# Third link of the block inverse in 64x64 products with a block diagonal operand, odd heads back from the exchanged halves one link sooner

## The chip, the cores and the metric

The kernel runs on one core of one Trainium2 chip. The metric is the device time of one execution in microseconds; lower is better. TensorE is written PE below, VectorE DVE, ScalarE ACT, GpSimd POOL, and the queue that issues most transfers SP.

## The reference, cut to what matters

A block of attention with a linear memory, followed by a gated MLP, for 4 sequences of 2048 tokens of width 256. The part that the change touches is the memory's delta rule: for each chunk of 64 tokens and each head, a strictly lower triangular 64x64 matrix is inverted, and the inverse corrects the values.

```
A0 = -jnp.where(strict, jnp.einsum('bnid,bnjd->bnij', wk, wk) * L[:, None], 0.0)
A = jnp.linalg.inv(eye - A0)
...
def step(S, inp):
    A_i, v_i, wk_i, rkg_i, wkg_i, intra_i = inp
    v_corr = A_i @ v_i
    wk_corr = A_i @ wk_i
    v_new = v_corr - wk_corr @ S
    o_i = rkg_i @ S + intra_i @ v_new
    S = gamma_C * S + wkg_i @ v_new
    return (S, o_i)
...
h = jax.nn.silu(_tlin(x, w1_w, w1_s)) * _tlin(x, w2_w, w2_s)
h = jax.nn.gelu(_tlin(h, h1_w, h1_s), approximate=False)
h = jax.nn.gelu(_tlin(h, h2_w, h2_s), approximate=False)
return _tlin(h, w3_w, w3_s)
```

## The kernel before, in words

The 32 chunks are 32 steps of a pipeline. In one step four sequences and four heads are worked on together: two sequences lie in partitions 0 to 63 and 64 to 127 (the chain `c`), and the 8 pairs of the other sequence bit and head are the index `m`, where `m` below `NP` = 4 are even heads (`e` = 0) and the rest odd heads (`e` = 1). So there are 16 matrices of 64x64 in a step, and each diagonal half of one is a 32x32 block; a 32 partition quarter is `quarter(c, i)`.

The order of the work is written out by hand in lists. `mixed` is the list of steps 3 to 33: the MLP of one chunk (`l1`, `l2` of this step, `l3` and `y` of the step before) is interleaved on PE with the small products of the memory for the next chunks. Each engine walks the same list and takes its own part of each item. A column of `l2` is 16 matmuls of 128x256. The items around the change come in this order in `mixed`: after column 7 of `l1` comes `lead`, after `l2` column 2 `join`, after `l2` column 4 `n` 3 and then `state`, after `l2` column 6 `attn_out`. `lead` and `join` serve two chunks: they finish one and start the inverse of the next.

The inverse of a 32x32 block is a product of three links. `lead` makes the first term (`first_term`, line 1120), DVE's `step_part` copies and transposes it. `join` makes square and term (`square_and_term`, line 1124) in quarters of 32x32, between the corner products (line 1146). DVE's `first_part` (lines 881, 882, 885) turns the square, subtracts the term, and adds the unit matrix. `n` 3 (line 1352) is the third link: 32 products of 32x32, one for each quarter of each matrix. ACT's `block_diagonal` (line 720) copies the result out of PSUM into `diag`, which holds the two 32x32 blocks of a matrix on a 64x64 diagonal. `state` follows at once on PE (lines 1420 and 1422), 32 products of 64x64.

A product whose operands lie in partition half `c` can write its result into the other half. In `mixed`, `first_term` does so for all heads, so that links one and two work in exchanged halves, and `move_inverse` has SP bring the block inverses into the exchanged halves too. The third link brings the result back.

PSUM tiles: `duo0` and `duo1` have two banks each, `solo0`, `solo1`, `mlp0`, `mlp1` one each. A product in fp32 is two LDWEIGHTS and two MATMUL in the trace; so 32 products of line 1352 are 64 rows there.

Of the kernel before, what the change touches and what calls it, by code (L numbers as in the profile page):

```python
# [22 lines left out]
F32 = mybir.dt.float32  # L23
# [3 lines left out]
ACT = mybir.ActivationFunctionType  # L27
# [3 lines left out]
P = 128  # L31
# [9 lines left out]
HB = C // 2  # L41
# [24 lines left out]
CO_TURN = CO_UP + C  # L66
CO_ROW = CO_TURN + P
CO_UNIT = CO_ROW + P
CO_N = CO_UNIT + HB


CHECKS = {0: (0,), 1: (1,), 2: (2, 3, 4), 3: (5,), 4: (6,), 5: (7, 8, 9, 10)}
# [5 lines left out]
def constants():  # L78

    c = np.zeros((P, CO_N), np.float32)  # L80
    p = np.arange(P)[:, None]
    j, i = p % C, np.arange(C)[None, :]
    c[:, CO_ID:CO_ID + P] = np.eye(P)
    c[:, CO_EYE:CO_EYE + SB] = j % SB == np.arange(SB)[None, :]
    c[:, CO_SUB:CO_SUB + HB // SB] = j % HB // SB == np.arange(HB // SB)[None, :]

    c[:, CO_MASK:CO_MASK + C] = (j // SB == i // SB) & (j > i)

    c[:, CO_MASK + C:CO_MASK + 2 * C] = (j // HB == i // HB) & (j // SB < i // SB)

    c[:, CO_MASK + 2 * C:CO_MASK + 3 * C] = (j >= HB) & (i < HB)
    c[:, CO_BLK:CO_BLK + 2] = j // HB == np.arange(2)[None, :]
    c[:, CO_UP:CO_UP + C] = i > j
    c[:, CO_DIST] = np.abs(p[:, 0] - (C - 1))

    c[:, CO_TURN:CO_TURN + P] = (p // C == p.T // C) & (j + j.T == C - 1)
    c[C - 1, CO_ROW:CO_ROW + P] = 1.0
    c[:, CO_UNIT:CO_UNIT + HB] = j % HB == np.arange(HB)[None, :]
    c[:, CO_E] = np.e
    return c  # L100


def half(k):
    return slice(C * k, C * k + C)
# [16 lines left out]
def main(nc, ctx, sb, sem, sems, x, wts, wv, wr, wmod, cT, scales, s3, decay, const, out):  # L121
# [30 lines left out]
    xin = sb("xin", [NB, D])  # L152
    last = sb("last", [NB, D])
    slot_low = sb("slot_low", [SLOTS // UNIT_SLOTS])
    any_low = sb("any_low", [1])
    row_low = sb("row_low", [1])


    NPAIR = H // 2
# [1 line left out]
    with ExitStack() as early:  # L161
        wmod_sb = sb("wmod_sb", [KT, 6 * D], F32, early)
        cT_sb = sb("cT_sb", [KT, B], F32, early)
        scT = sb("scT", [KT, B], F32, early)
        scB = sb("scB", [KT, B, C], F32, early)
        s3_sb = sb("s3_sb", [KT], F32, early)
        gate_col = sb("gate_col", [2, KT, B], F32, early)
        sgn = sb("sgn", [2, KT, B], F32, early)
        mag = sb("mag", [2, KT, B], F32, early)
        gate_cols = sb("gate_cols", [2, KT, B, C], F32, early)  # L170
        dec = sb("dec", [NPAIR + H + NPAIR], F32, early)
        gam = sb("gam", [NPAIR + H + NPAIR], F32, early)
        edec = sb("edec", [NPAIR + H + NPAIR], F32, early)
        powers = sb("powers", [H], F32, early)
        pow_row_sb = sb("pow_row_sb", [P], F32, early)
        hank = sb("hank", [H, C], F32, early)
        low_bits = sb("low_bits", [UNIT_SLOTS * SLOT * P], F32, early)
    act_hi = [sb(f"act_hi{i}", [HK, TOK], F32R) for i in range(2)]
    act_lo = [sb(f"act_lo{i}", [HK, TOK], F32R) for i in range(2)]
# [42 lines left out]
    mi = sb("mi", [2 * NP, HB])  # L222
    step_nt = sb("step_nt", [2 * NP, HB])
    square_t = sb("square_t", [2 * NP, HB])
    first_two = sb("first_two", [2 * NP, HB])
    vn = sb("vn", [NP, 2, DH])
    o_state = sb("o_state", [NP, P])
# [244 lines left out]
    with nc.Block() as block:  # L472
# [238 lines left out]

        @block.scalar
        def _(act):
            def block_diagonal(a):

                act.wait_ge(rest_full, a + 1)
                after(act, own_full, a)
                after(act, mi_full, a)
                for i in range(2):
                    ins = act.activation(diag[:, :, HB * i:HB * (i + 1)], of_head(duo[1][:, 1, 0:2 * NP * HB]), ACT.Copy, scale=con[:, CO_BLK + i:CO_BLK + i + 1])  # L720
                ins.then_inc(diag_ready, 1)

            def new_values(a):
# [3 lines left out]
            def step(n, g, items):  # L727
                def part(name, k, a, p):
# [31 lines left out]
                        for e in range(2):  # L760
                            act.copy(gram[:, e], grams(a, e)[:, :, 0:C]).then_inc(gram_ready[e], 1)
                    if name == "n" and k == 3:
                        block_diagonal(a)
                    if name == "lead" or name == "solve" and k == 0:
                        act.wait_ge(own_full, now)
                        act.copy(vn[:].rearrange("p q e n -> p (q e n)"), solo[1][:]).then_inc(own_ready, 1)
# [66 lines left out]
        def _(dve):  # L833
# [45 lines left out]
            def first_part(a):  # L879
                dve.wait_ge(first_full, a + 1)  # L880
                dve.transpose(square_t[:].rearrange("p k n -> p (k n)"), duo[1][:, 0, 0:2 * NP * HB]).then_inc(square_turned, 1)
                dve.tensor_tensor(first_two[:], first_inv_t, of_head(duo[1][:, 0, 2 * NP * HB:4 * NP * HB]), ALU.subtract).then_inc(first_ready, 1)
                dve.wait_ge(const_in, 16)
                dve.wait_ge(square_turned, a + 1)
                dve.tensor_tensor(square_t[:], square_t[:], con[:, CO_UNIT:CO_UNIT + HB].unsqueeze(1).to_broadcast([P, 2 * NP, HB]),
                                  ALU.add).then_inc(square_ready, 1)

            def step_part(a):
                dve.wait_ge(step_full, a + 1)
# [3 lines left out]
            def step(n, g, items):  # L893
# [4 lines left out]
                def part(name, k, a, p):  # L898
# [68 lines left out]
                    if name == "lead" and (not isinstance(n, int) or n + 1 < STEPS):  # L967
                        step_part(n + 1)
                    if name == "n" and k == 2:
                        first_part(a)  # L970
                    if name == "join" and (not isinstance(n, int) or n + 1 < STEPS):
                        first_part(n + 1)
# [141 lines left out]
        def _(pe):  # L1114
# [7 lines left out]
            def square_and_term(m, rows):  # L1122

                return pe.matmul(duo[1][rows, 0, :].rearrange("p (t k n) -> p t k n", t=2, n=HB)[:, :, m, :], step_nt[rows, m, :],  # L1124
                                 step_and_inv[rows, :, m, :], start=True, stop=True)

            def inner(m, c):

# [25 lines left out]
            def step(general, n, g, items):  # L1154
# [86 lines left out]
                def part(name, k, a, p):  # L1241
# [86 lines left out]
                    if name == "n":  # L1328
                        pe.wait_ge(const_in, 16)
                        if k == 1:  # L1330
                            pe.wait_ge(cross_ready, now)
                            pe.wait_ge(inv_ready, now)
                            if items is third:
                                pe.wait_ge(state_ready, a)
                        if k == 2:
                            pe.wait_ge(step_ready, now)
                            pe.wait_ge(inv_t_ready, now)
                            if items is third:
                                pe.wait_ge(ao_scaled, a)
# [6 lines left out]
                        for e, q, c, i in quarters if k > 1 else ():  # L1346
                            rows, m = quarter(c, i), e * NP + q
                            if k == 2:
                                mm = square_and_term(m, rows)
                            if k == 3:  # L1350
                                back = quarter(1 - c if items is mixed else c, i)
                                mm = pe.matmul(of_head(duo[1][back, 1, 0:2 * NP * HB])[:, m, :], square_t[rows, m, :], first_two[rows, m, :], start=True, stop=True)  # L1352
                        mm.then_inc({1: step_full, 2: first_full, 3: rest_full}[k], 1)
                    if name == "join":
                        has_next = not isinstance(n, int) or n + 1 < STEPS
                        pe.wait_ge(const_in, 16)
                        if has_next:
                            pe.wait_ge(step_ready, n + 2)
                        pe.wait_ge(mi_ready, now)
                        pe.wait_ge(own_ready, now)  # L1360
                        pe.wait_ge(o_state_ready, a)

                        for e in range(2):
                            for q in range(NP):
                                m = e * NP + q
                                for c in range(2):
                                    last_corner = corner(m, e, q, c)
                                if has_next:
                                    for i in range(2):
                                        for c in range(2):  # L1370
                                            last_terms = square_and_term(m, quarter(c, i))
                        last_corner.then_inc(vn_full, 1)
                        if has_next:
                            last_terms.then_inc(first_full, 1)
# [50 lines left out]
                    if name == "attn_out":  # L1425
                        if items is alone:
                            pe.wait_ge(wr_ready, 1)
                        pe.wait_ge(oT_ready, now)
                        for b in range(NB):
                            for hp in range(H // 2):  # L1430
# [84 lines left out]
```

## Time and profile before

| | before |
|---|---|
| median of 3 runs | 1748.63 us |
| lowest and highest | 1748.12 and 1750.38 us |
| the profiled execution's own time | 1744.08 us |
| its span, first to last instruction | 1742.3 us |
| granted PE clock over the span | 0.991 |
| PE busy | 1716.0 us, 98% |
| DVE, ACT, POOL busy | 64%, 55%, 34% |

A step in the middle is 52.0 us long. Start times in a timeline are from the span's start; "x64" is the number of instructions that the row merges. A matmul's own duration includes the way through the array, and matmuls overlap, so what a group costs is the time from its first start to the first start of the next group.

### The profile page before, as it was taken

What the parts mean: (1) busy time and instruction counts of PE and PEld (TensorE: products, weight loads), DVE (VectorE), ACT (ScalarE), POOL (GpSimd) and SP (SyncE); (2) the same over time, 40 slices, a digit from 0 to 9 for tenths busy, and PEclk for the clock granted to TensorE, in tenths of its full rate; (3) what the DMA queues carried; (4) which work ended last, traced back from release to release, by engine and by line L of the source; (5) the groups of instructions that cost most, each with busy time, mean ns of one, the idle gap of its engine ahead of it and who ended that gap; (6) DMA issues with size and microseconds to landing.
All of it is one profiled execution on the core that took longest, in us unless ns stands there. A gap on an engine that the chain in (4) does not pass through costs nothing.

```text
span 1742.3 us, 60528 instructions
## 1 busy us (share of the span) xinstructions
PE 1716.0 (98%) x25488; PEld 1651.6 (95%) x25488; DVE 1115.4 (64%) x3041; ACT 963.3 (55%) x2249; POOL 593.5 (34%) x694
## 2 busy tenths in 40 slices
PE   8799999999999999999999999999999999999999
PEld 5698999999999999999999999999999999999998
DVE  5677666666666666676666676666666666666432
ACT  4664555555555555555555555555555555565554
POOL 3544333343333343333243333243233243243101
PEclk8899999999999999999999999999999999999999
DMA  8101000000000000000000000000000000000000
GB/s 291 68 14 33 12 23 23 18 20 11 24 23 23 18 20 11 24 23 24 17 21 15 20 23 23 20 17 19 16 23 23 21 17 21 14 23 17 8 3 12
DMA packets 37356, 47.08 MB, mean 27 GB/s; under 512 B 9236, under 2 KB 29336, under 8 KB 37080
## 3 DMA queue, kind: packets, MB, share of 16 engines
q1 hardware_dynamic: 35088, 40.75, 8.4%
q8 instruction: 206, 3.38, 0.8%
q10 hardware_dynamic: 1992, 2.38, 0.5%
q14 instruction: 70, 0.57, 0.1%
HBM read 22.53 MB, written 8.39 MB: 18 GB/s over the span
## 4 chain that ended last, share of the span: by engine, by line
PE 93%; DVE 1%; issue 1%; POOL 1%; ACT 1%; DVEq 0%; POOLq 0%
PE mlp L1163 64%; PE mlp L1235 6%; PE solo L1163 3%; PE duo L1431 3%; PE solo L1304 3%; PE solo L1136 2%; PE duo L1352 1%; PE duo L1129 1%; PE duo L1420 1%; PE solo L1440 1%; PE duo L1124 1%; PE duo L1325 1%; PE solo L1146 1%; PE duo L1422 1%; PE duo L1316 1%
## 5 line engine op out<-in xcount | busy, mean ns | idle before, releaser
L1163 PE MATMUL mlp<-act_hi,w_hi 128*128 128x256 f32 x4096 | 968.0, 283 | 1.1 <-POOL act_lo L668 0.6
L1163 PE MATMUL mlp<-act_lo,w_hi 128*128 128x256 f32 x4096 | 945.2, 277 | 0.0
L1163 PEld LDWEIGHTS mlp<-act_hi,w_hi 128*128 128x128 f32 x4096 | 770.1, 188 | 9.8 <-POOL act_lo L668 1.3
L1163 PEld LDWEIGHTS mlp<-act_lo,w_hi 128*128 128x128 f32 x4096 | 770.4, 188 | 0.8
L805 ACT ACTIVATE full<-mlp,scale_sb 128x256 f32<-128x256 f32 x512 | 246.4, 481 | 553.7 <-PE mlp L1163 553.5
L895 DVE TENSOR_TENSOR act_lo<-full,act_hi 128x256 fp32r<-128x256 f32 x512 | 240.2, 469 | 321.7 <-ACT act_hi L806 319.1
L668 POOL TENSOR_TENSOR act_lo<-full,act_hi 128x256 fp32r<-128x256 f32 x256 | 186.6, 735 | 501.9 <-ACT act_hi L795 501.9
L806 ACT ACTIVATE act_hi<-mlp,scale_sb 128x256 fp32r<-128x256 f32 x512 | 242.6, 474 | 0.0
L1163 PE MATMUL mlp<-xh,w_hi 128*128 128x256 f32 x768 | 190.8, 286 | 3.5 <-issue 3.0
L1163 PE MATMUL mlp<-xl,w_hi 128*128 128x256 f32 x768 | 189.8, 282 | 0.0
L607 POOL TENSOR_TENSOR rstd<-ve,minus_half 128x2 f32<-128x2 f32 x64 | 49.1, 768 | 331.7 <-DVE ve L844 331.3
L1014 DVE SCALAR_TENSOR_TENSOR full<-mlp,scale_sb,gate 128x256 f32<-128x256 f32 x192 | 92.8, 484 | 99.2 <-ACT gate L790 96.8
L1163 PEld LDWEIGHTS mlp<-xh,w_hi 128*128 128x128 f32 x768 | 145.9, 190 | 5.1 <-issue 4.2
L790 ACT ACTIVATE gate<-mlp,scale_sb 128x256 f32<-128x256 f32 x192 | 91.0, 474 | 107.7 <-PE mlp L1163 107.7
L1163 PEld LDWEIGHTS mlp<-xl,w_hi 128*128 128x128 f32 x768 | 146.2, 190 | 0.0
L1235 PE MATMUL mlp<-w_hi,act_hi 128*128 128x256 f32 x512 | 118.2, 277 | 0.0
L1235 PE MATMUL mlp<-w_hi,act_lo 128*128 128x256 f32 x512 | 118.1, 276 | 0.0
L607 POOL TENSOR_TENSOR rinv<-ssm,minus_half 128x8 f32<-128x8 f32 x32 | 52.8, 1650 | 182.2 <-DVE ssm L873 182.2
L795 ACT CAST act_hi<-full 128x256 fp32r<-128x256 f32 x256 | 101.7, 397 | 10.6 <-DVE full L1014 10.6
L1235 PEld LDWEIGHTS mlp<-w_hi,act_hi 128*128 128x128 f32 x512 | 96.1, 188 | 0.1
L1235 PEld LDWEIGHTS mlp<-w_hi,act_lo 128*128 128x128 f32 x512 | 96.1, 188 | 0.0
L779 ACT ACTIVATE h<-solo,sbm,cb 128x64 f32<-128x64 f32 x256 | 84.0, 438 | 0.3 <-PE solo L1440 0.3
(179 smaller groups left out, 2679.9 us busy)
## 6 DMA issues: line engine op xcount, KB each, us to landing
w_raw<-in_wts SPq DMA_DIRECT2D x22, 512.0 KB, 5.0
kg<-r SPq DMA_DIRECT2D x64, 126.0 KB
xin<-in_x SPq DMA_DIRECT2D x62, 128.0 KB
out_y<-y SPq DMA_DIRECT2D x62, 128.0 KB, 2.5
step_and_inv<-square_t SPq DMA_DIRECT2D x56, 64.0 KB, 2.0
wmod_sb<-in_wmod ACTq DMA_DIRECT2D x1, 1024.0 KB, 9.1
kg<-last SPq DMA_DIRECT2D x64, 2.0 KB
last<-r SPq DMA_DIRECT2D x64, 2.0 KB, 1.7
```

The source lines that it names most:

```text
L607: pool.tensor_tensor(dst[:], src[:], minus_half[:, 0:src.shape[1]], ALU.pow).then_inc(done, 1)
L668: pool.tensor_tensor(act_lo[0][:, k, :], full[k % 3][:], act_hi[0][:, k, :].bitcast(F32), ALU.subtract).then_inc(l_ready[0], 1)
L779: ins = act.activation(h2[:].rearrange("p k b n -> p (k b n)")[:, cols], solo[1][:, cols], ACT.Identity, bias=sbm[:, k, b:b + 1], scale=cb ...
L790: act.activation(gate[k % 2][:], gated[k % 3][:, 0:TOK], ACT.Silu, scale=scale_sb[:, 0, k:k + 1]).then_inc(l_act[0], 1)
L795: act.copy(act_hi[0][:, j, :], full[j % 3][:]).then_inc(l1_hi, 1)
L805: act.activation(full[k % 2][:], mlp[k % 2][:, 0:TOK], ACT.Gelu, scale=s)
L806: act.activation(act_hi[layer % 2][:, k, :], mlp[k % 2][:, 0:TOK], ACT.Gelu, scale=s).then_inc(l_act[layer], 1)
L895: dve.tensor_tensor(act_lo[layer % 2][:, k, :], full[k % 2][:], act_hi[layer % 2][:, k, :].bitcast(F32), ALU.subtract).then_inc(l_ready[la ...
L1014: dve.scalar_tensor_tensor(full[k % 3][:], up, s, gate[k % 2][:], ALU.mult, ALU.mult).then_inc(prod_ready, 1)
L1163: mm = pe.matmul(dst, *general_ops, start=is_first and i == 0, stop=is_last and i == 1)
L1235: mm = pe.matmul(mlp[k][:, 0:D], *ops, start=j == 0 and i == 0, stop=j == HK - 1 and i == 1)
L1304: mm = pe.matmul(solo[0][:, b * D:(b + 1) * D], hT[:, kt, b, :], wv_sb[:, kt, :], start=kt == 0, stop=kt == KT - 1)
```

## The change

Only steps whose list is `mixed` change in their work, in four ways.

- In `join`, the square and the term go to `duo0` instead of `duo1`: even heads to its first bank, odd heads to its second. The odd heads' products write into the other partition half, so that they are back where they belong one link sooner.
- DVE's `first_part` subtracts the terms of even and odd heads apart (each from the inverse that lies in its half), turns the two squares apart into `inv`, and writes `square_d`, a block diagonal 64x64 operand, in two instructions that multiply by a mask and add a masked unit matrix.
- The third link is 16 products with a 64x64 stationary operand and 32 moving columns, in place of 32 products of 32x32. Even heads go from exchanged halves to their own, odd heads stay; even heads write the first bank of `duo1`, odd heads the second.
- ACT's `block_diagonal` reads the two banks, and `attn_out`, whose result goes into the first bank of `duo1`, waits for it (`diag_ready`).

The constants get 64 more columns; `any_low` and `row_low` move into the memory that is given back after the start, and `square_d` takes new memory.

```
-                dve.transpose(square_t[:].rearrange("p k n -> p (k n)"), duo[1][:, 0, 0:2 * NP * HB]).then_inc(square_turned, 1)
-                dve.tensor_tensor(first_two[:], first_inv_t, of_head(duo[1][:, 0, 2 * NP * HB:4 * NP * HB]), ALU.subtract).then_inc(first_ready, 1)
+                if turned:
+                    for e, own_inv in ((0, first_inv_t), (1, square_t)):
+                        ms = slice(NP * e, NP * e + NP)
+                        term = duo[0][:, e, NP * HB:2 * NP * HB].rearrange("p (k n) -> p k n", n=HB)
+                        ins = dve.tensor_tensor(first_two[:, ms], own_inv[:, ms], term, ALU.subtract)
+                    ins.then_inc(first_ready, 1)
+                    for e in range(2):
+                        ins = dve.transpose(inv[:, NP * e:NP * e + NP].rearrange("p k n -> p (k n)"), duo[0][:, e, 0:NP * HB])
+                    ins.then_inc(square_turned, 1)
...
                 dve.wait_ge(square_turned, a + 1)
-                dve.tensor_tensor(square_t[:], square_t[:], con[:, CO_UNIT:CO_UNIT + HB].unsqueeze(1).to_broadcast([P, 2 * NP, HB]),
-                                  ALU.add).then_inc(square_ready, 1)
+                if turned:
+                    for i in range(2):
+                        unit_i = con[:, CO_UNIT + HB * (i + 1):CO_UNIT + HB * (i + 2)].unsqueeze(1).to_broadcast([P, 2 * NP, HB])
+                        ins = dve.scalar_tensor_tensor(square_d[:, :, HB * i:HB * (i + 1)], inv[:], con[:, CO_BLK + i:CO_BLK + i + 1], unit_i, ALU.mult, ALU.add)
+                    ins.then_inc(square_ready, 1)
...
+            def square_and_term_back(m, c, i):
+
+                to = quarter(c if m < NP else 1 - c, i)
+                return pe.matmul(duo[0][to, m // NP, 0:2 * NP * HB].rearrange("p (t k n) -> p t k n", t=2, n=HB)[:, :, m % NP, :], step_nt[quarter(c, i), m, :],
+                                 step_and_inv[quarter(c, i), :, m, :], start=True, stop=True)
...
+                        for q in range(NP) if k == 3 and items is mixed else ():
+                            for c in range(2):
+                                for m in (q, NP + q):
+                                    back = 1 - c if m < NP else c
+                                    mm = pe.matmul(duo[1][half(back), m // NP, m % NP * HB:(m % NP + 1) * HB], square_d[half(c), m, :], first_two[half(c), m, :],
+                                                   start=True, stop=True)
...
-                                            last_terms = square_and_term(m, quarter(c, i))
+                                            last_terms = square_and_term_back(m, c, i)
...
+                        if items is mixed and (not isinstance(n, int) or n + 1 < STEPS):
+                            pe.wait_ge(diag_ready, n + 2)
```

PE's program around the third link in a mixed step, before; the rows of column 4 of `l2` stand above it, `state` below. A row is one instruction, or as many as its "x" says, and counts products, not their two passes.

```order
1109 L1163 MATMUL mlp0<-act_lo0,w_full 128x256
1110 L1352 MATMUL duo1<-first_two,square_t 32x32 [waits first_ready,square_ready,const_in]
1111 L1352 MATMUL duo1<-first_two,square_t 32x32 x31
1112 L1420 MATMUL duo0<-intra1,vn 64x64 [waits vn_ready,kg_ready,const_in]
1113 L1420 MATMUL duo0<-intra1,vn 64x64 x15
1114 L1422 MATMUL duo0<-vn,kg1 64x64 x16
...
1149 L1431 MATMUL duo1<-wr_turned,o_state 128x256 [waits oT_ready]
```

And the same place after the change:

```order
1109 L1191 MATMUL mlp0<-act_lo0,w_full 128x256
1110 L1378 MATMUL duo1<-first_two,square_d 64x32 [waits first_ready,square_ready,const_in]
1111 L1378 MATMUL duo1<-first_two,square_d 64x32 x15
1112 L1453 MATMUL duo0<-intra1,vn 64x64 [waits vn_ready,kg_ready,const_in]
1113 L1453 MATMUL duo0<-intra1,vn 64x64 x15
1114 L1455 MATMUL duo0<-vn,kg1 64x64 x16
...
1149 L1466 MATMUL duo1<-wr_turned,o_state 128x256 [waits oT_ready,diag_ready]
```

The 32 products have become 16 and nothing else moved; `attn_out` has one wait more.

DVE's program from the `l2` column before `first_part` on, in the same step, before:

```order
397 L895 TENSOR_TENSOR act_lo1<-full0,act_hi1 128x256 [waits l_act1]
398 L881 STREAM_TRANSPOSE square_t<-duo1 128x256 [waits first_full]
399 L882 TENSOR_TENSOR first_two<-step_and_inv,duo1 128x256
400 L885 TENSOR_TENSOR square_t<-square_t,con 128x256 [waits square_turned,const_in]
401 L410 REGISTER_ALU [waits h_ready]
402 L869 TENSOR_TENSOR r<-h 128x512 [waits last_in]
```

And after the change:

```order
397 L917 TENSOR_TENSOR act_lo1<-full0,act_hi1 128x256 [waits l_act1]
398 L891 TENSOR_TENSOR first_two<-step_and_inv,duo0 128x128 [waits first_full]
399 L891 TENSOR_TENSOR first_two<-square_t,duo0 128x128
400 L894 STREAM_TRANSPOSE inv<-duo0 128x128 x2
401 L904 SCALAR_TENSOR_TENSOR square_d<-inv,con 128x8x32 [waits square_turned,const_in]
402 L904 SCALAR_TENSOR_TENSOR square_d<-inv,con 128x8x32
403 L414 REGISTER_ALU [waits h_ready]
404 L875 TENSOR_TENSOR r<-h 128x512 [waits last_in]
```

Three instructions have become six, and what follows them is the same.

## Rows read from the trace of the kernel before

**Rows 1.** The page: busy time by engine, PE's clock and DMA rate in 40 slices, one costly group.

```profile
PE 1716.0 (98%) x25488; PEld 1651.6 (95%) x25488; DVE 1115.4 (64%) x3041; ACT 963.3 (55%) x2249; POOL 593.5 (34%) x694
...
PEclk8899999999999999999999999999999999999999
...
GB/s 291 68 14 33 12 23 23 18 20 11 24 23 23 18 20 11 24 23 24 17 21 15 20 23 23 20 17 19 16 23 23 21 17 21 14 23 17 8 3 12
...
L1014 DVE SCALAR_TENSOR_TENSOR full<-mlp,scale_sb,gate 128x256 f32<-128x256 f32 x192 | 92.8, 484 | 99.2 <-ACT gate L790 96.8
```

**Rows 2.** Busy time of each engine in one mixed step, from link to link.

```profile
1045.55:1097.55 52.00, 52.00 (x797) 50.60 (x796) 34.43 (x94) 28.95 (x69) 18.08 (x22) 1.00 0.08 20
```

**Rows 3.** All that PE waited for between 210 and 1620 us, longest first.

```profile
PE duo L1120 <- issue: 0.7, 2, 0.4
PE mlp L1163 <- issue: 0.3, 1, 0.3
```

**Rows 4.** Timeline of PE around one third link: start, length, group.

```profile
1045.55 0.75 PE L1352 MATMUL duo<-first_two,square_t 32*32 32x32 f32 x64
1046.24 0.69 PE L1420 MATMUL duo<-intra,vn 64*64 64x64 f32 x32
1046.75 0.65 PE L1422 MATMUL duo<-vn,kg 64*64 64x64 f32 x32
1047.33 0.38 PE L1163 MATMUL mlp<-act_hi,w_hi 128*128 128x256 f32 x1
```

**Rows 5.** The link's group over the whole span, and the first and last mixed link.

```profile
L1352 PE MATMUL duo<-first_two,square_t x2048: 183/191/213, 38.6 to 1619.3; 32*32 32x32 f32 x187
...
213.03 0.75 PE L1352 MATMUL duo<-first_two,square_t 32*32 32x32 f32 x64
...
214.23 0.65 PE L1422 MATMUL duo<-vn,kg 64*64 64x64 f32 x32
...
1618.78 0.75 PE L1352 MATMUL duo<-first_two,square_t 32*32 32x32 f32 x64
...
1619.98 0.65 PE L1422 MATMUL duo<-vn,kg 64*64 64x64 f32 x32
```

**Rows 6.** Timeline of PE in the second half of one lead.

```profile
1033.95 0.23 PE L1129 MATMUL duo<-diag,far 64*64 64x32 f32 x2
1033.96 0.23 PE L1120 MATMUL duo<-inv,cross 64*64 64x32 f32 x2
1034.01 0.23 PE L1129 MATMUL duo<-diag,far 64*64 64x32 f32 x2
...
1034.77 0.23 PE L1129 MATMUL duo<-diag,far 64*64 64x32 f32 x2
```

**Rows 7.** Timeline of PE: first group of one join, and the matmul after it.

```profile
1040.59 0.24 PE L1146 MATMUL solo<-vn,mi 32*32 32x64 f32 x2
...
1041.71 0.39 PE L1163 MATMUL mlp<-act_hi,w_hi 128*128 128x256 f32 x1
```

**Rows 8.** Timeline of DVE from the first part on; in brackets idle before, and releaser.

```profile
1041.91 0.44 DVE L881 STREAM_TRANSPOSE square_t<-duo 128x256 f32<-128x256 f32 x1
1042.28 0.38 DVE L882 TENSOR_TENSOR first_two<-step_and_inv,duo 128x256 f32<-128x256 f32 x1
1042.59 0.41 DVE L885 TENSOR_TENSOR square_t<-square_t,con 128x256 f32<-128x256 f32 x1
1042.91 0.68 DVE L869 TENSOR_TENSOR r<-h 128x512 f32<-128x512 f32 x1
...
1044.72 0.43 DVE L895 TENSOR_TENSOR act_lo<-full,act_hi 128x256 fp32r<-128x256 f32 x1 [0.20 <-ACT act_hi L806]
1046.53 0.42 DVE L895 TENSOR_TENSOR act_lo<-full,act_hi 128x256 fp32r<-128x256 f32 x1 [1.39 <-ACT act_hi L806]
```

**Rows 9.** Timelines: ACT's block diagonal, and PE's first matmul of attn_out.

```profile
1046.39 0.84 ACT L720 ACTIVATE diag<-duo,con 128x256 f32<-128x256 f32 x2
...
1051.08 0.59 PE L1431 MATMUL duo<-wr_turned,o_state 128*128 128x256 f32 x2
```

More of the change, by code:

```diff
@@ L68 @@
 CO_UNIT = CO_ROW + P
-CO_N = CO_UNIT + HB
+CO_N = CO_UNIT + 3 * HB
 CHECKS = {0: (0,), 1: (1,), 2: (2, 3, 4), 3: (5,), 4: (6,), 5: (7, 8, 9, 10)}
@@ L98, in constants @@
     c[:, CO_UNIT:CO_UNIT + HB] = j % HB == np.arange(HB)[None, :]
+    for half_of in range(2):
+        c[:, CO_UNIT + HB * (half_of + 1):CO_UNIT + HB * (half_of + 2)] = (j % HB == np.arange(HB)[None, :]) & (j // HB == half_of)
     c[:, CO_E] = np.e
@@ L154, in main @@
     slot_low = sb("slot_low", [SLOTS // UNIT_SLOTS])
-    any_low = sb("any_low", [1])
-    row_low = sb("row_low", [1])
     NPAIR = H // 2
@@ L176, in main @@
         hank = sb("hank", [H, C], F32, early)
+        any_low = sb("any_low", [1], F32, early)
+        row_low = sb("row_low", [1], F32, early)
         low_bits = sb("low_bits", [UNIT_SLOTS * SLOT * P], F32, early)
@@ L224, in main @@
     square_t = sb("square_t", [2 * NP, HB])
+    square_d = sb("square_d", [2 * NP, C])
     first_two = sb("first_two", [2 * NP, HB])
@@ L713, in _, with block_diagonal @@
         def _(act):
-            def block_diagonal(a):
+            def block_diagonal(a, turned):
+                rest = (duo[1][:, :, 0:NP * HB].rearrange("p e (q n) -> p e q n", n=HB) if turned else
+                        duo[1][:, 1, 0:2 * NP * HB].rearrange("p (e q n) -> p e q n", e=2, n=HB))
                 act.wait_ge(rest_full, a + 1)
@@ L719, in block_diagonal @@
                 for i in range(2):
-                    ins = act.activation(diag[:, :, HB * i:HB * (i + 1)], of_head(duo[1][:, 1, 0:2 * NP * HB]), ACT.Copy, scale=con[:, CO_BLK + i:CO_BLK + i + 1])
+                    ins = act.activation(diag[:].rearrange("p (e q) n -> p e q n", e=2)[:, :, :, HB * i:HB * (i + 1)], rest, ACT.Copy, scale=con[:, CO_BLK + i:CO_BLK + i + 1])
                 ins.then_inc(diag_ready, 1)
@@ L762, in part @@
                     if name == "n" and k == 3:
-                        block_diagonal(a)
+                        block_diagonal(a, items is mixed)
                     if name == "lead" or name == "solve" and k == 0:
@@ L877, in norm, with first_part @@
                                       rinv[:].unsqueeze(2).to_broadcast([P, NB * H, DH]), ALU.mult).then_inc(r_ready, 1)
-            def first_part(a):
+            def first_part(a, turned):
                 dve.wait_ge(first_full, a + 1)
-                dve.transpose(square_t[:].rearrange("p k n -> p (k n)"), duo[1][:, 0, 0:2 * NP * HB]).then_inc(square_turned, 1)
-                dve.tensor_tensor(first_two[:], first_inv_t, of_head(duo[1][:, 0, 2 * NP * HB:4 * NP * HB]), ALU.subtract).then_inc(first_ready, 1)
+                if turned:
[7 more added lines that the diff above has]
+                    ins.then_inc(square_turned, 1)
+                else:
+                    dve.transpose(square_t[:].rearrange("p k n -> p (k n)"), duo[1][:, 0, 0:2 * NP * HB]).then_inc(square_turned, 1)
+                    dve.tensor_tensor(first_two[:], first_inv_t, of_head(duo[1][:, 0, 2 * NP * HB:4 * NP * HB]), ALU.subtract).then_inc(first_ready, 1)
@@ L883, in first_part @@
                 dve.wait_ge(const_in, 16)
                 dve.wait_ge(square_turned, a + 1)
-                dve.tensor_tensor(square_t[:], square_t[:], con[:, CO_UNIT:CO_UNIT + HB].unsqueeze(1).to_broadcast([P, 2 * NP, HB]),
-                                  ALU.add).then_inc(square_ready, 1)
+                if turned:
[3 more added lines that the diff above has]
+                    ins.then_inc(square_ready, 1)
+                else:
+                    dve.tensor_tensor(square_t[:], square_t[:], con[:, CO_UNIT:CO_UNIT + HB].unsqueeze(1).to_broadcast([P, 2 * NP, HB]),
+                                      ALU.add).then_inc(square_ready, 1)
@@ L969, in part @@
                     if name == "n" and k == 2:
-                        first_part(a)
+                        first_part(a, False)
                     if name == "join" and (not isinstance(n, int) or n + 1 < STEPS):
-                        first_part(n + 1)
+                        first_part(n + 1, True)
                     if name == "state":
@@ L1345, in part @@
                                 mm = first_term(m, c, c)
-                        for e, q, c, i in quarters if k > 1 else ():
+                        for q in range(NP) if k == 3 and items is mixed else ():
[4 more added lines that the diff above has]
+                                                   start=True, stop=True)
+                        for e, q, c, i in quarters if k == 2 or k == 3 and items is not mixed else ():
                             rows, m = quarter(c, i), e * NP + q
@@ L1350, in part @@
                             if k == 3:
-                                back = quarter(1 - c if items is mixed else c, i)
-                                mm = pe.matmul(of_head(duo[1][back, 1, 0:2 * NP * HB])[:, m, :], square_t[rows, m, :], first_two[rows, m, :], start=True, stop=True)
+                                mm = pe.matmul(of_head(duo[1][rows, 1, 0:2 * NP * HB])[:, m, :], square_t[rows, m, :], first_two[rows, m, :], start=True, stop=True)
                         mm.then_inc({1: step_full, 2: first_full, 3: rest_full}[k], 1)
```

## The prediction

> **What bounds the kernel now.** I read the page first. PE is busy 98% of the span, DVE 64%, ACT 55%, POOL 34%, and PE's clock stands in the page's top tenth in all but the first two slices [rows 1], so of its two levels, 1.2 and 2.4 GHz, it holds the upper. Then the view of windows, for one mixed step: 52.00 us long, with 52.00 us of PE busy, against 34.43 of DVE [rows 2]. Then the waits of PE over all the mixed steps: 1.0 us in three pieces, none of them put down to another engine [rows 3]. So from 210 to 1620 us the kernel's time is the length of PE's own stream of instructions. What is worth anything there is what shortens that stream; other engines matter only where they become so late that PE meets them. The page's busy PE is no measure of a single group, since matmuls overlap: I use the time from a group's first start to the next group's first start.
>
> **What the third link costs now.** In the timeline the link starts at 1045.55 and the first product of `state` at 1046.24: 0.69 us for 32 products, 64 instructions. The two groups of `state`, 16 products of 64x64 each, take 1046.24 to 1046.75 (0.51 us) and 1046.75 to 1047.33 (0.58 us) [rows 4]. Link and first half of `state` together take 1.20 us here, 214.23 - 213.03 = 1.20 in the first mixed link, and 1619.98 - 1618.78 = 1.20 in the last [rows 4, 5]. The link has 2048 instructions in all [rows 5], 32 links of 64; four of them belong to the first four chunks, whose lists don't change. 28 links change.
>
> **What it will cost.** The new link is 16 products with 64 stationary and 32 moving columns, 32 instructions. That shape stands in the trace, in the second half of `lead`: `inner` and `first_term` are 64x64 products with 32 moving columns. There instructions start in bursts of four (two of line 1129, two of line 1120), one for each of the four 64x64 tiles of the array: `inner` stays in its partition half, `first_term` crosses. From 1033.95 to 1034.77 there are 14 such bursts, 0.059 us each; a burst follows 0.06 us on the one before [rows 6]. 32 instructions are 8 bursts: 8 x 0.059 = 0.47 us.
>
> Where it stands, it takes over the start-up of `state`. 8 bursts of `state` cost 8 x 0.059 = 0.47 us at that pace, but its first group takes 0.51 [rows 4]; so entering 64x64 products costs 0.04 more than the pace. Now the link pays that and `state` runs on in the same shape. Link and first group of `state` become 0.51 + 0.47 = 0.98 us in place of 1.20: **0.22 us less in a step**.
>
> Here a rule of the Trainium skill speaks to the sum ("TensorEngine Tiling (Array Packing)", Key Properties): changing the tiling mode drains the engine. Before, the link is in 32x32 tiles and `state` in 64x64; after, there is no change of mode between them. By the rule the drain goes away. No run here shows its price alone.
>
> 28 x 0.22 = 6.2 us.
>
> **The other parts.**
>
> `join` keeps its 48 products. From 1040.59 to 1041.71 it takes 1.12 us [rows 7]. For the odd heads the terms now go from quarters 0, 1, 2, 3 to 2, 3, 0, 1 in place of straight through. With the corners (0 to 1 and 2 to 3) they use six different tiles as before, each input quarter and each output quarter as often as before. The old third link itself crossed halves in just this way, at 0.69 us for 64 instructions, 0.011 each, which is no slower than `join` now: 96 instructions in 1.12, 0.012 each [rows 4, 7]. So I take nothing; the nearest bound above is one burst more for each of the four odd `m`, 4 x 0.059 = 0.24 us a step. A gain I exclude, since nothing is taken out.
>
> DVE's `first_part` is 1042.91 - 1041.91 = 1.00 us now: transpose 0.37, subtraction 0.31, addition 0.32, start to start [rows 8]. After: two subtractions and two transposes on half the columns, and two full instructions of the three-operand kind. The trace shows no half size. Lower bound of the halves, half a full one each: 0.31 + 0.37 = 0.68; upper bound, a full one each: 1.36. The two full ones lie between the addition's 0.32 and the 0.484 us of the three-operand kind reading PSUM [rows 1, 8]: 0.64 to 0.97. Sum 1.3 to 2.3 us; I take 1.7, as the fixed part of an instruction doesn't halve. It is then done at 1043.6, at the latest 1044.3 (1041.91 + 2.3), and PE wants it at 1045.55 [rows 4, 8]. Slack 1.9 us, at the least 1.2. Nothing on PE is late.
>
> What is late next is DVE's queue: `r`, its sum and floor, and the `act_lo` of an `l2` column, which starts at 1044.72 after 0.20 us of idle time; the next one starts at 1046.53 after 1.39 us idle [rows 8]. So 0.7 us (at most 1.3) of lateness dies in 0.20 + 1.39 us of idle time, before `state` gives DVE its two additions. That one `act_lo` would be half a microsecond late; it feeds `l3`, long after. The link itself can't start before PE has done column 4, whatever DVE does. Were that cover gone, each 0.1 us beyond it would cost 2.8 us over 28 steps.
>
> The new wait of `attn_out` on `diag_ready`: ACT's block diagonal runs from 1046.39 to 1047.23, the first matmul of `attn_out` starts at 1051.08 [rows 9]: 3.8 us to spare. All of PE's stream is queued behind it, but it costs nothing. ACT reads the same number of columns from two banks in place of one: same price.
>
> The constants grow by 64 columns of 128 rows, 32 KB in the start. At the 291 GB/s of the first slice [rows 1] that is 0.11 us if it is wholly exposed, 0 if not. I take 0.1. SP's and POOL's queues don't change in a step.
>
> **The sum.** 6.2 - 0.1 = 6.1 us. The profiled execution took 1744.08 us with a span of 1742.3; this gives 1738.0 and 1736.2. The median of the runs, 1748.63, lies 4.55 above the profiled execution, and the same stream runs in both; so I forecast 1748.63 - 6.1 = 1742.5 us. A change is told from none here from 0.2% on, 3.5 us.
>
> **Rivals.**
>
> 1. *Same-half neighbours queue up (slower).* In `lead`, the two products that follow one another in the program start from different partition halves. In the new link they start from the same half: half 0 to 1, half 0 to 0, half 1 to 0, half 1 to 1. If such a pair can't overlap, 8 bursts become 16: 0.47 us more, so 1.20 becomes 1.45, +0.25 a step, 28 x 0.25 = +7 us: 1755.6. It turns from gain to loss at 0.22 / 0.059, about four extra bursts. Against it: in the bursts of `lead` all four tiles start within 0.02 us, two of them from each half [rows 6], which is what this rival forbids. 5%. The Trainium skill has a rule with the same outcome (same page, Restrictions and Gotchas, Gotcha 1): different row tiles can't access the same PSUM bank at once. As a mechanism of this kernel: even heads of both halves write bank 0 of `duo1`, odd heads of both bank 1, so a burst would split in two, with the same 1755.6 by the rows. The trace disagrees: in the bursts of `lead`, `inner` of both halves writes one bank and `first_term` of both another, at 0.059 us for four [rows 6]. 2%.
>
> 2. *The join gives it back (no change).* If the crossing terms of the odd heads take one burst more for each `m`, 28 x 0.24 = 6.6 us are lost: 1749.1, no change. For it: they share the stream with corners, which the old crossing link did not. Against it: the tile counts above. A half of this (a burst for every other `m`) gives 1745.8. Together 13%, mostly the former.
>
> 3. *The first part comes late.* It needs 3.6 us in place of 1.0 before PE waits at 1045.55; the upper bound is 2.3. At 4 us it would cost 0.4 x 28 = 11 us: 1753.7. 1%.
>
> 4. *Less gain from the link itself.* If the burst with its new row order takes 0.065 in place of 0.059, or the start-up is paid a second time, 0.05 to 0.09 us are missing: 1743.9 to 1745.0. This is within the likeliest case's edge.
>
> **How the numbers follow.** The forecast's case (8 bursts, join unchanged, DVE hidden) has 79%, rival 4 in it; rival 2 13%, rivals 1 and 3 with the rule 8%. Of the 79%, a small gain below 3.5 us has about 1%. Faster by over 0.2%: 0.79; within: 0.13 (rival 2 and that remainder); slower: 0.08. The range goes below the forecast by 2.3 us: 1.1 if the start-up of 0.04 vanishes altogether (28 x 0.04), 0.5 by which the lowest run lies under the median, and 0.7 of the 1.0 us that PE shows as issue [rows 3], if the shorter code saves it. It goes above to 1746, past rival 4 and the half of rival 2. 1740.2 to 1746.0.
>
> **What would show it.** Right: the link in 28 x 32 = 896 instructions where there were 1792, in bursts of four every 0.059 us; link to second group of `state` about 0.98 us; `join` 1.12; a mixed step 51.78 us with PE busy throughout; no wait of PE for `square_d` or `diag`; DVE busier by 0.7 us a step. Wrong: link bursts of two, or 0.9 us long (rival 1 or the bank rule); `join` at 1.3 (rival 2); a PE wait released by DVE line 904 (rival 3).

## The result

| | before | after |
|---|---|---|
| median | 1749.03 us (6 runs, 1746.1 to 1751.02) | 1777.74 us (6 runs, 1776.86 to 1780.61) |
| span of the profiled execution | 1742.3 us | 1777.7 us |
| ratio of the times | | 1.0168, 95% interval 1.0154 to 1.0181 |

The change makes the kernel 1.7% slower, 28.7 us by the medians. The forecast was 1742.5 us.

The page of the changed kernel, busy time by engine and PE's clock, answers to [rows 1]:

```profile
PE 1748.0 (98%) x24592; PEld 1683.3 (95%) x24592; DVE 1133.4 (64%) x3125; ACT 964.1 (54%) x2249; POOL 598.6 (34%) x694
...
PEclk8899999999999999999999999999999999999999
```

PE executes 896 instructions fewer, as predicted, and is busy for 32 us longer, at the same granted clock. One mixed step, from link to link (view of windows, answers to [rows 2]):

```profile
1014.24:1067.35 53.11, 53.11 (x765) 51.75 (x765) 35.05 (x97) 28.98 (x69) 18.25 (x22) 1.00 0.08 20
```

1.11 us longer, with PE busy in all of it. So no wait to speak of has appeared, and the view of PE's waits from 210 to 1650 us says so too; it answers to [rows 3]:

```profile
PE duo L1142 <- issue: 1.4, 2, 0.9
PE mlp L1263 <- DVE act_lo L917: 0.3, 1, 0.3
PE mlp L1191 <- issue: 0.3, 1, 0.3
```

That is 2.0 us in all, 1.0 more than before, out of 28.7.

Each piece that the change edits does what the prediction said, within the sizes given at the end. Timeline of PE around one join and the link behind it; answers to [rows 4] and [rows 7]:

```profile
1062.25 0.24 PE L1174 MATMUL solo<-vn,mi 32*32 32x64 f32 x2
...
1063.37 0.38 PE L1191 MATMUL mlp<-act_hi,w_hi 128*128 128x256 f32 x1
...
1067.35 0.67 PE L1378 MATMUL duo<-first_two,square_d 64*64 64x32 f32 x32
1067.84 0.67 PE L1453 MATMUL duo<-intra,vn 64*64 64x64 f32 x32
1068.33 0.65 PE L1455 MATMUL duo<-vn,kg 64*64 64x64 f32 x32
```

The join takes 1.12 us, as before. Link and first group of `state` take 1068.33 - 1067.35 = 0.98 us in place of 1.20; it is 0.98 in all 28 links of this trace, and 1.20 in all 28 before. The timeline of DVE, which answers to [rows 8]:

```profile
1063.57 0.28 DVE L891 TENSOR_TENSOR first_two<-step_and_inv,duo 128x128 f32<-128x128 f32 x1
...
1063.96 0.51 DVE L894 STREAM_TRANSPOSE inv<-duo 128x128 f32<-128x128 f32 x2
1064.58 0.88 DVE L904 SCALAR_TENSOR_TENSOR square_d<-inv,con 128x256 f32<-128x256 f32 x2
1065.38 0.68 DVE L875 TENSOR_TENSOR r<-h 128x512 f32<-128x512 f32 x1
```

1.81 us from the first start to the start of `r`, and done 1.9 us before PE's link at 1067.35.

What has become longer is what the change doesn't edit: the dense matmuls of the MLP. They are easiest to compare in the chain that ended last, which merges runs of one line (start, length, group, number of matmuls). Before:

```profile
1010.80 10.90 PE mlp L1163 x96
1021.70 3.63 PE mlp L1235 x32
1025.33 1.92 PE mlp L1163 x16
...
1087.00 5.66 PE mlp L1163 x48
```

After:

```profile
1031.64 11.52 PE mlp L1191 x96
1043.16 3.80 PE mlp L1263 x32
1046.96 1.87 PE mlp L1191 x16
...
1056.42 5.89 PE mlp L1191 x48
```

In this order the rows are six columns of `l3`, the 32 matmuls of `y`, two columns of `l1`, and three columns of `l2`. `l3` goes from 10.90 / 96 = 113.5 to 11.52 / 96 = 120.0 ns a matmul, `y` from 113.4 to 118.8, `l2` takes 0.23 / 48 = 4.8 ns more; `l1` alone is faster, 0.05 / 16 = 3.1 ns. Times 128, 32, 128 and 64 matmuls in a step: 0.83 + 0.17 + 0.61 - 0.20 = 1.41 us more, less 0.22 for the link: 1.19, where the windows show 1.11.

`l2`, `l3` and `y` multiply the weights `w_hi` with `act_hi` and `act_lo`, `l1` with `xh` and `xl`. Their shapes, order and neighbours are as before. What differs is where these tensors lie in SBUF. The change adds 256 bytes of constants per partition ahead of them, takes out 64 (`any_low`, `row_low`, for which the allocation gives 32 each), and puts 2048 (`square_d`) between `act` and `x`. So the `act` tiles moved by 192 bytes and `xh`, `xl` by 2240; `w_hi` lies ahead of all this and did not move. The table gives the byte in a partition at which each tensor starts in the built programs. "Distance" below is the difference between such a byte and that of `w_hi`; a block of weights is 512 bytes wide and the blocks of the other operand lie 1024 apart, so modulo 512 it is the same for every matmul of a layer.

| bytes | w_hi | act tiles | xh, xl | act - w_hi, modulo 256 | x - w_hi, modulo 256 |
|---|---|---|---|---|---|
| before | 1152 | 123200 and multiples of 8192 above | 211680, 213728 | 192 | 96 |
| after | 1152 | 123392 and so on | 213920, 215968 | 128 | 32 |

### The profile page after: what moved, and what is told of

The parts are those of the page before. It is cut to its first block, busy times and chain, and to the rows that moved or that the text cites. A ratio compares the mean times of both kernels' runs of the same rounds, so it can differ in the third digit from the quotient of the medians.

```text
span 1777.7 us, 58848 instructions
## 1 busy us (share of the span) xinstructions
PE 1748.0 (98%) x24592; PEld 1683.3 (95%) x24592; DVE 1133.4 (64%) x3125; ACT 964.1 (54%) x2249; POOL 598.6 (34%) x694
## 4 chain that ended last, share of the span: by engine, by line
PE 94%; DVE 2%; issue 1%; POOL 1%; DMA 1%; ACT 0%; ACTq 0%; DVEq 0%; POOLq 0%
PE mlp L1191 64%; PE mlp L1263 7%; PE solo L1191 3%; PE duo L1466 3%; PE solo L1332 3%; PE solo L1164 2%; PE duo L1157 1%; PE duo L1353 1%; PE solo L1475 1%; PE solo L1174 1%; PE duo L1378 1%; PE duo L1152 1%; PE duo L1453 1%; PE duo L1344 1%; PE duo L1455 1%
## 5 line engine op out<-in xcount | busy, mean ns | idle before, releaser
L1191 PE MATMUL mlp<-act_hi,w_hi 128*128 128x256 f32 x4096 | 1006.3, 287 | 0.9 <-POOL act_lo L672 0.6
L1191 PE MATMUL mlp<-act_lo,w_hi 128*128 128x256 f32 x4096 | 984.5, 283 | 0.3 <-issue 0.3
L1191 PE MATMUL mlp<-xh,w_hi 128*128 128x256 f32 x768 | 185.9, 282 | 3.3 <-issue 2.8
L1191 PE MATMUL mlp<-xl,w_hi 128*128 128x256 f32 x768 | 185.1, 280 | 0.0
L1263 PE MATMUL mlp<-w_hi,act_hi 128*128 128x256 f32 x512 | 123.0, 282 | 0.3 <-DVE act_lo L917 0.3
L1263 PE MATMUL mlp<-w_hi,act_lo 128*128 128x256 f32 x512 | 123.1, 282 | 0.0
## 6 DMA issues: line engine op xcount, KB each, us to landing
wmod_sb<-in_wmod ACTq DMA_DIRECT2D x1, 1024.0 KB, 10.3
```

Of the source, the lines that this page charges most:

```text
L1191: mm = pe.matmul(dst, *general_ops, start=is_first and i == 0, stop=is_last and i == 1)
L1263: mm = pe.matmul(mlp[k][:, 0:D], *ops, start=j == 0 and i == 0, stop=j == HK - 1 and i == 1)
```

## The experiments

**Theory A:** the pace of the dense matmuls depends on where their operands `act` and `x` lie in SBUF; the change is a gain of some 6 us, and the shift of the tiles a loss on top. **Theory B, the rival:** something in the new instructions (crossing join, two-bank link, heavier DVE part) slows all of PE's stream.

**1. The change in full, tiles back in their places.** Tensors with 192 bytes move from the front of SBUF to its end.

```diff
-    scale_sb = sb("scale_sb", [4, HK])
-    minus_half = sb("minus_half", [NB * H])
-    flag_i = sb("flag_i", [1], I32)
...
     w_full = sb("w_full", [SLOT, P])
+    scale_sb = sb("scale_sb", [4, HK])
+    minus_half = sb("minus_half", [NB * H])
+    flag_i = sb("flag_i", [1], I32)
```

> The changed kernel in full, with three small tensors (scale_sb, minus_half, flag_i, 192 bytes together) moved from the front of SBUF to its end, so that act_hi, act_lo, xh and xl lie where they lay in the kernel before (act tiles at the same byte, xh and xl 2048 bytes higher). Theory A (where the moving operands lie in SBUF sets the pace of the dense matmuls): about 1743 us, the old median less 6; matmuls on act_hi and act_lo every 114 ns, link slot still 0.49. Theory B (something that the new instructions do, the crossing join, the two-bank link or the heavier DVE part, slows all of PE's stream): about 1778 us, matmuls every 119 to 120 ns.

Measured: 1741.98 us against 1748.29 of before on the same chip, ratio 0.9964 (0.9952 to 0.9976). The chain shows the old lengths:

```profile
1007.89 10.90 PE mlp L1191 x96
...
1022.42 1.92 PE mlp L1191 x16
```

and the timeline of PE the new link, with 0.48 us to the first product of `state`:

```profile
1042.63 0.67 PE L1378 MATMUL duo<-first_two,square_d 64*64 64x32 f32 x32
1043.11 0.67 PE L1453 MATMUL duo<-intra,vn 64*64 64x64 f32 x32
```

A mixed step, from link to link, was to take 51.78 us by the prediction:

```profile
990.94:1042.63 51.69, 51.69 (x765) 50.33 (x765) 34.98 (x98) 28.94 (x69) 18.11 (x22) 1.00 0.08 20
```

Theory A's number, and theory B is out: all of the change's instructions are in this kernel. By the interval of the ratio the gain lies between 4 and 8 us.

**2. The kernel before, in the changed kernel's places.**

```diff
-CO_N = CO_UNIT + HB
+CO_N = CO_UNIT + 3 * HB
...
     square_t = sb("square_t", [2 * NP, HB])
+    pad = sb("pad", [2 * NP, C])
```

(`any_low` and `row_low` move to the early tensors as in the change.)

> The kernel before, no instruction of the change in it, but with the changed kernel's places in SBUF: 64 more columns of constants, any_low and row_low among the early tensors, and an unused tensor of square_d's size. Theory A: 1784 to 1788 us, six and more above the changed kernel, since it keeps the old link; act matmuls every 119 to 120 ns. Theory B: 1749 us, as before.

Measured: 1782.87 us, ratio 1.0203 (1.0189 to 1.0217) to the same runs of before. Its `l3` run, the same row of the chain:

```profile
1032.87 11.52 PE mlp L1164 x96
```

So the loss comes without a single instruction of the change. Moving the tensors costs 34.6 us (1782.87 - 1748.29), and in the old places the change gains 6.3 (1748.29 - 1741.98).

**3 and 4. One group of tiles at a time.** An unused tensor of 192 bytes ahead of `act_hi0`, with 320 more behind the `act` tiles; or 192 ahead of `xh`.

```diff
+    pad0 = sb("pad0", [48])
     act_hi = [sb(f"act_hi{i}", [HK, TOK], F32R) for i in range(2)]
     act_lo = [sb(f"act_lo{i}", [HK, TOK], F32R) for i in range(2)]
+    pad1 = sb("pad1", [80])
```

> The kernel before with act_hi and act_lo alone 192 bytes higher; all that lies behind them is 512 bytes higher. Theory A, with the place within 512 bytes as what counts: act matmuls 119 to 120 ns in place of 114, xh and xl matmuls unchanged at 118 to 122, in all 1791 to 1797 us. If the place counts in another way (the distance between xh and act, say) this comes out elsewhere. Theory B: 1749 us.

> The kernel before with xh, xl and what lies behind them (gate, full, y) 192 bytes higher, act tiles where they were. Theory A: act matmuls unchanged at 114 ns, xh and xl matmuls at 116 to 118 ns in place of 118 to 122, in all about 1742 us. Theory B: 1749 us.

Measured: 1788.81 us, ratio 1.023 (1.0215 to 1.0246), for `act` alone; 1744.39, ratio 0.9977 (0.9967 to 0.9987), for `x`. The first, two to eight microseconds less than expected, carries the whole loss, with `l1` left as it was; its rows of the chain:

```profile
1090.02 11.52 PE mlp L1165 x96
1101.55 3.84 PE mlp L1237 x32
1105.38 1.92 PE mlp L1165 x16
```

The second gains 3.9 us, where I had expected 6 to 7. Its `l1` is as fast as in the changed kernel, but in each step one pair of `l2` columns has become slower. Two steps of its chain; in each the first row of 32 is the pair after `join`, the second the pair after `state`:

```profile
1030.14 1.87 PE mlp L1164 x16
...
1043.58 3.84 PE mlp L1164 x32
1049.20 3.97 PE mlp L1164 x32
...
1095.44 3.98 PE mlp L1164 x32
1101.19 3.85 PE mlp L1164 x32
```

In the kernel before the pair after `join` takes 3.84 us, and the pair after `state`

```profile
1047.40 3.85 PE mlp L1163 x32
```

So some 0.13 us of each step are lost again, and from step to step the slow pair changes places. The `act` tiles and the weights lie here as in the kernel before: their distance alone can't explain it. `gate`, `full` and `y` lie behind `xh` and moved with it; that one of them, written while `l2` runs, is the cause was not tried.

**5. Place or distance?** An unused tensor of 192 bytes ahead of everything, the weights too.

```diff
+    pad0 = sb("pad0", [48])
     with ExitStack() as before:
         w_raw = sb("w_raw", [BLOCKS, P], F32, before)
```

> The kernel before with everything, the weights w_hi too, 192 bytes higher in SBUF. The act tiles lie at the same byte as in the shifted run (0 modulo 512), but their distance to the weights is that of the kernel before. If the distance between moving operand and weights is what counts: 1749 us, act matmuls every 114 ns, x matmuls 118 to 122. If the place of the moving operand itself counts (a boundary of 512 bytes): about 1783 us, act matmuls every 119 ns.

Measured: 1745.05 us, before 1745.14, ratio 0.9999 (0.9988 to 1.001). The `act` tiles are at the bytes where they cost 40 us in experiment 3, and here they cost nothing (chain):

```profile
1010.95 10.90 PE mlp L1164 x96
1021.85 3.63 PE mlp L1236 x32
1025.48 1.92 PE mlp L1164 x16
```

So the place by itself is out, at least for a shift of 192 bytes, and what counts is a distance between tensors. This run keeps all distances, so it doesn't say to which tensor; experiments 1, 3 and 4 narrow that. In 1 most of what lies between the constants and `act` (masks, `state`, `rT` and others) moves against `act` by 64 or 128 bytes, and the pace is the old one. In 3 the distance from `act` to `x` changes and the pace of `l1` doesn't (1.92 us for 16); in 4 `x`, `gate`, `full` and `y` move against `act` and the pace of `l3` and `y` doesn't (10.90 and 3.63 us). The weights are the one other tensor in SBUF that these matmuls read, and I take the distance to them as the cause. The few tensors just behind `w_hi` (`wv_sb`, `wr_turned`, the constants) never moved against it; no dense matmul reads them.

**6 to 9. Four sweeps.** The kernel before, with unused tensors between the tiles, so that `l2` and `y` (they read `act_hi0`, `act_lo0`), `l3` (`act_hi1`, `act_lo1`) and `l1` have a distance each. The first one; in the others the four sizes differ:

```diff
+    pad0 = sb("pad0", [64])
+    act_hi, act_lo = [], []
+    for i in range(2):
+        if i == 1:
+            pad1 = sb("pad1", [16])
+        act_hi.append(sb(f"act_hi{i}", [HK, TOK], F32R))
+        act_lo.append(sb(f"act_lo{i}", [HK, TOK], F32R))
+    pad2 = sb("pad2", [48])
...
+    padx = sb("padx", [24])
     xh = sb("xh", [KT, TOK], F32R)
```

> The kernel before with three distances to the weights (modulo 512) in one kernel: the act tiles that l2 and y read at 448, those that l3 reads at 0, xh and xl at 192. If distance or place counts alone, the x matmuls fall to 114 ns, the pace of the act tiles at 192 in the kernel before. For 448 and 0 no number is known; both theories expect them slower than 114, since less distance means that weights and operand are read from neighbouring places at one time.

> As the run before it, with l2's act tiles at distance 64, l3's at 128, xh and xl at 384. At 384 the act tiles took 119 to 120 ns; if the tile doesn't matter but its distance does, xh and xl take that too. 64 and 128 lie on both sides of 96, where xh and xl took 117 to 123 ns: I expect about 118 to 122.

> As the runs before it, with l2's act tiles at distance 256, l3's at 320, xh and xl at 0. 288 gave xh and xl 116 to 118 ns, so I expect 115 to 119 for both act pairs. This run and the two before it show whether any distance beats 192.

> The kernel before with l2's act tiles at distance 160 to the weights (modulo 256), l3's at 224, xh and xl at 224. So far 192 gave 113.4 to 114.6 for act tiles, 64 gave 116 to 118, and 0 and 128 gave 118.8 to 119.9. If the best place is a narrow one, both act pairs are over 115 here; if it is a wide one, they stay at 114.

One run of each: 1762.58, 1774.6, 1790.7 and 1779.13 us, against 1745.14 (the last 1745.06) of before. From their chains, first, second, third and fourth sweep:

```profile
987.01 1.81 PE mlp L1170 x16
...
1039.48 1.88 PE mlp L1170 x16
...
1074.14 11.51 PE mlp L1170 x96
1085.65 3.63 PE mlp L1242 x32
1098.82 5.64 PE mlp L1170 x48
```

```profile
1052.78 5.64 PE mlp L1170 x48
...
1059.54 3.96 PE mlp L1170 x32
...
1080.95 11.52 PE mlp L1170 x96
1092.47 3.77 PE mlp L1242 x32
```

```profile
1049.21 3.84 PE mlp L1242 x32
1062.71 5.95 PE mlp L1170 x48
...
1091.31 11.31 PE mlp L1170 x96
```

```profile
1055.89 5.89 PE mlp L1170 x48
...
1084.26 11.36 PE mlp L1170 x96
1095.62 3.83 PE mlp L1242 x32
```

Ordered by distance, with the runs above, lengths in us for the number of matmuls given:

| distance modulo 512 | modulo 256 | l3, 96 | y, 32 | l2, 48 | l1, 16 |
|---|---|---|---|---|---|
| 192 (before) | 192 | 10.90 | 3.63 | 5.66 | 1.88, in some steps 1.81 |
| 448 | 192 | | 3.63 | 5.64 | 1.88, in some steps 1.81 |
| 64 | 64 | | 3.77 | 5.64 | |
| 320 | 64 | 11.31 | | | |
| 0 | 0 | 11.51 | | | 1.92 |
| 256 | 0 | | 3.84 | 5.95 | |
| 128 | 128 | 11.52 | | | |
| 384 (after, experiment 3) | 128 | 11.52 | 3.80, 3.84 | 5.89 | 1.90 |
| 160 | 160 | | 3.83 | 5.89 | |
| 224 | 224 | 11.36 | | | 1.89 |
| 96 (`x` before) | 96 | | | | 1.92 |
| 288 (`x` after) | 32 | | | | 1.87 |

192 and 448 agree within 0.02 us in `y`, `l2` and `l1`, 128 and 384 in `l3`. That speaks for a period of 256 bytes; 64 and 320, 0 and 256 have no column in common and say nothing on it. 192 is best in `l3` and `y`, and 32 bytes from it (160 for `y`, 224 for `l3`) some three quarters of the gain or more are gone: it is a narrow place. In `l2` 64 is as good for the first run of a step, but the pairs after `join` and `state` take 3.96 and 3.97 us in the step shown, and 3.84 and 3.85 in the kernel before (after `join` it is 3.83 in 14 of the 26 middle steps). In `l1` 192 and 288 are equal.

The distance doesn't set the pace alone. At the same 192 `l3` takes 113.5 ns a matmul, `l2` 5.66 / 48 = 118 and, after the join, 3.84 / 32 = 120, and `l1` in most steps 1.88 / 16 = 117.5. And at one distance of 384, `y` takes 3.80 us in one kernel and 3.84 in another.

Misses: I expected `l1` to fall to 114 ns at 192. It does in 7 of the 26 middle steps of the first sweep (1.81 us for 16, 113), and in the others it takes 1.88; what sets these steps apart is open. I expected 448 to be slower than 114 ns, and `y` takes 3.63 / 32 = 113.4 there. And of 115 to 119 at 256 and 320, 256 gave 3.84 / 32 = 120.

**10. Order of the link's products.** Rival 1 of the prediction, tested in the good places.

```diff
-                            for c in range(2):
-                                for m in (q, NP + q):
+                            for m in (q, NP + q):
+                                for c in range(2):
```

> The changed kernel in the old places, with the link's 16 products in another order: neighbours start from different partition halves (as in lead), where the change has two in a row start from the same half. If the order matters (my rival 1), the link slot falls below the 0.49 us that the change has. If four tiles run side by side in any order, it stays 0.49 us and the total 1742 us.

Measured: one time, 1739.79 us. Its timeline of PE has 0.49 us from the link to `state`:

```profile
1041.75 0.67 PE L1378 MATMUL duo<-first_two,square_d 64*64 64x32 f32 x32
1042.24 0.67 PE L1453 MATMUL duo<-intra,vn 64*64 64x64 f32 x32
```

The slot is 0.49 us in every one of the 28 links, as in the changed kernel's own order. For the link the order doesn't matter.

**11. The change with the best places for all tiles.** As experiment 1, and `st2`, `mv2`, `ve2`, `rstd2` (160 bytes) moved to the end, so that `xh` and `xl` lie at distance 192 too.

```diff
-    st2 = sb("st2", [NB, 6])
-    mv2 = sb("mv2", [NB, 2])
-    ve2 = sb("ve2", [NB])
-    rstd2 = sb("rstd2", [NB])
```

> The changed kernel with its act tiles where they lay before (distance 192 to the weights, modulo 256) and, new, xh and xl at distance 192 too: four small tensors (st2, mv2, ve2, rstd2, 160 bytes) moved to the end of SBUF on top of the three of the first run. The sweep gave l1 116.8 ns a matmul at 192 and 120.0 at 96, its place so far: 64 matmuls x 3.2 ns x 31 steps = 6.3 us. Theory A: 1742.0 - 6.3 = 1735.7 us, the fastest of all. If the gain of x is taken back in l2, as l2's 0.9 ns when gate, full and y moved by 192, it ends at about 1738. Theory B says nothing here.

Measured: 1734.79 us against 1745.06 of before, ratio 0.9939 (0.9925 to 0.9954). It beats both kernels, the one before by 10.3 us, the changed one by 2.2% (0.9939 / 1.0168). Its chain:

```profile
1004.93 10.90 PE mlp L1191 x96
...
1019.45 1.89 PE mlp L1191 x16
```

That the time lies so near to the 1735.7 expected is in part luck. The sum started from 1742.0, which was measured beside a before of 1748.29, and this one beside 1745.06. Told as a gain over the kernel before, I had expected 6.3 + 6.3 = 12.6 us, and 10.3 came: 4.0 from the places of `xh` and `xl` instead of 6.3. `l1` went from 1.92 to 1.88 or 1.89 us for 16 matmuls, which is 3.7 to 5.0 us over 31 steps; the slow pair of `l2` columns of experiment 4 isn't there.

## Why the prediction was wrong

The step that failed is in the first part and in "The other parts": "What is worth anything there is what shortens that stream", with the edits' own instructions as all that could change its length. The prediction took the price of every instruction that isn't edited as fixed. It even named the 256 bytes of constants ("The constants grow by 64 columns of 128 rows"), and costed them as a transfer at the start, 0.1 us, and not for where they push what lies behind them. No rival had the dense matmuls in it, though line 1163 alone is 64% of the chain on the page of before; its three layers and `y` make up most of a step, and 4 to 6% on all but `l1` outweighs any link. What the runs showed in its place: with the tensors shifted, the untouched matmuls of `l3` take 120.0 ns in place of 113.5, those of `y` and `l2` some 5 ns more, which is 34.6 us lost by the shift alone (experiment 2), 6.3 gained (experiment 1), together 28.3, and the result is 28.7.

Point by point:

- *The link*: 1.20 to 0.98 us with the first group of `state`, as worked out. The split is another: 0.49 and 0.49, where 0.51 and 0.47 had been said. The sum, 6.1 us, is 6.3 in experiment 1.
- *The mode change*: what the rule of the Trainium skill ("TensorEngine Tiling (Array Packing)", Key Properties) speaks of was in that sum through the row with the first group. The 0.22 us agree with it, but its price alone was not tried.
- *Rival 1 and the bank rule*: rival 1 had the slot at 0.47 us more. It is 0.49 us in the change's order and in the other (experiment 10), with both partition halves writing the same bank in a burst. Neither rival 1 nor the rule of the Trainium skill (same page, Restrictions and Gotchas, Gotcha 1) cost anything here.
- *Rival 2*: the join is 1.12 us before and after.
- *DVE*: 1.81 us where 1.7 was taken within 1.3 to 2.3. No wait of PE for it; slack 1.9 us. Among PE's waits one on a later `act_lo` of DVE is new (0.3 us in all, 0.9 in experiment 1); that DVE's longer part caused it was not tried.
- *`attn_out`'s new wait*: nothing of it among PE's waits, and ACT's two copies take 0.84 us as before.
- *Start*: not told apart; the middle of the kernel explains the difference.

What stays open is the mechanism. The runs show that the pace goes with the distance between the two operands (experiments 3 to 9), with a period that looks like 256 bytes, and that something besides it has a part, as the slow pair of `l2` columns (experiment 4) and the different paces at 192 show. That the weight load of the next matmul and the operand stream of the current one meet in the same part of SBUF would fit, but no run looks at that, and it doesn't say why 192 is better than 64.

## What to carry to other kernels

Where one engine's stream is the bound, an edit has two prices: its own instructions, and what its memory does to the places of all operands behind it. So compare the tensor addresses of the two programs before costing anything, and keep the hot operands' places fixed (new tensors behind them, or padding). When a time moves and no wait does, compare the length of equal runs of untouched instructions first; and when they differ, run the old kernel with the new layout. That one run separates layout from edit.

## What the runs showed of the hardware that was not expected

A 128x128 by 128x256 matmul in fp32r, back to back on this chip at the full granted clock, takes 113.5 to 120.0 ns, and the byte distance between stationary and moving operand within a partition decides much of it: 10.90 against 11.52 us for 96 matmuls of `l3`, with 192 modulo 256 the best of the distances tried. The same distance didn't bring every layer to 113.5 ns (`l2` stayed at 118 to 120, `l1` at 117.5 in most steps). The effect shows with the weights stationary (`l2`, `l3`) and with them moving (`y`, 3.63 against 3.84 us for 32). Over this kernel the `act` tiles' distance is worth 40.5 us (1788.81 against 1748.29).
